# First layer of a two-layer graph transformer: scores by 32-row tiles in four shared PSUM banks, and a new order of the softmax work on VectorE

## The reference

```
q, k, v = x @ wq + bq, x @ wk + bk, x @ wv + bv        # 8 heads of 48
scores  = einsum('bhqd,bhkd->bhqk', q, k) * 48**-0.5 + adj
ctx     = softmax(scores) @ v
x       = rmsnorm(x + ctx @ wo + bo)
x       = rmsnorm(x + silu(x @ w1 + b1) @ w2 + b2)      # 384 -> 1536 -> 384
```

## Time and profile before

| | |
|---|---|
| median of 3 runs | 2001.8 us (2001.61 to 2002.91) |
| profiled execution | 2003.69 us, its span 2001.9 us |
| PE, DVE, ACT, POOL busy | 96%, 67%, 54%, 21% of the span |
| granted TensorE clock, mean | 0.983 |

### The profile page before, as it was taken

The page is one execution under the profiler, slowest core; times in us unless marked ns, Lnnn a source line. Parts: engine busy times, 40 slices in busy tenths (PEclk is TensorE's granted clock), DMA queues, the critical chain, the costliest instruction groups (busy, mean ns, idle before and its releaser), DMA issues.

```text
span 2001.9 us, 50636 instructions
## 1 busy us (share of the span) xinstructions
PE 1928.2 (96%) x18496; PEld 1879.4 (94%) x18496; DVE 1339.1 (67%) x2590; ACT 1088.6 (54%) x2326; POOL 413.6 (21%) x555
## 2 busy tenths in 40 slices
PE   6599999999999999999999999999799999999997
PEld 5589999999999999999999999998799999999997
DVE  6547667766667666676676766764566766666765
ACT  4346555565555655556555565544355555555555
POOL 3011212212112121121211312122122221222222
PEclk9699999999999999999999999999899999999999
DMA  7424444443444444434444344344222222222222
GB/s 191 138 79 119 114 120 121 109 121 111 115 126 108 118 115 112 129 107 119 115 108 133 105 121 115 105 121 111 75 76 87 86 80 71 85 84 87 87 79 65
DMA packets 268645, 213.54 MB, mean 107 GB/s; under 512 B 142784, under 2 KB 251072, under 8 KB 268608
## 3 DMA queue, kind: packets, MB, share of 16 engines
q1 hardware_dynamic: 268608, 213.05, 38.7%
HBM read 120.34 MB, written 79.69 MB: 100 GB/s over the span
## 4 chain that ended last, share of the span: by engine, by line
PE 92%; DVE 3%; DMA 2%; SPq 1%; ACT 1%; issue 1%; POOL 0%; ACTq 0%; POOLq 0%; DVEq 0%
PE a_bank L405 59%; PE b_bank L1243 15%; PE b_banks L1243 5%; PE a_bank L476 3%; PE b_bank L1310 2%; PE a_bank L461 2%; PE b_banks L1297 2%; PE b_banks L1287 2%; PE b_bank L1320 1%; SPq L247 1%; DMA a_hid_stage<-in_L_gnn_w 1%; DMA a_work<-x_turned 1%; DMA x_turned<-a_work 0%; DVE xt_lo L792 0%; DVE a_work L875 0%
## 5 line engine op out<-in xcount | busy, mean ns | idle before, releaser
L405 PE MATMUL a_bank<-a_x1t_hi,a_w_hi 128*128 128x256 f32 x1152 | 329.5, 286 | 9.8 <-DVE a_x1t_lo L807 8.3
L405 PE MATMUL a_bank<-a_x1t_lo,a_w_hi 128*128 128x256 f32 x1152 | 326.2, 283 | 0.0
L405 PE MATMUL a_bank<-a_x1t_hi,a_w_lo 128*128 128x256 f32 x1152 | 326.1, 283 | 0.0
L657 ACT ACTIVATE a_work<-a_bank,a_b 128x256 f32<-128x256 f32 x384 | 159.8, 467 | 240.2 <-PE a_bank L405 239.9
L822 DVE TENSOR_TENSOR a_hid_lo<-a_work,a_hid_hi 128x512 fp32r<-128x512 f32 x192 | 130.8, 694 | 195.3 <-ACT a_hid_hi L662 195.3
L405 PE MATMUL a_bank<-a_w_hi,a_hid_hi 128*128 128x384 f32 x768 | 258.3, 336 | 0.0
L405 PE MATMUL a_bank<-a_w_hi,a_hid_lo 128*128 128x384 f32 x768 | 258.2, 336 | 0.0
L405 PE MATMUL a_bank<-a_w_lo,a_hid_hi 128*128 128x384 f32 x768 | 258.1, 336 | 0.0
L405 PEld LDWEIGHTS a_bank<-a_x1t_hi,a_w_hi 128*128 128x128 f32 x1152 | 219.7, 191 | 18.7 <-issue 9.9
L405 PEld LDWEIGHTS a_bank<-a_x1t_lo,a_w_hi 128*128 128x128 f32 x1152 | 222.5, 193 | 0.0
L405 PEld LDWEIGHTS a_bank<-a_x1t_hi,a_w_lo 128*128 128x128 f32 x1152 | 219.3, 190 | 0.0
(11 more groups left out here) (160 smaller groups left out, 5591.4 us busy)
## 6 DMA issues: line engine op xcount, KB each, us to landing
a_work<-in_x SPq DMA_DIRECT2D x64, 384.0 KB, 3.2
p_turned<-a_work SPq DMA_DIRECT2D x256, 64.0 KB, 1.8
a_work<-p_turned SPq DMA_DIRECT2D x32, 512.0 KB, 3.2
xt_raw<-in_xT SPq DMA_DIRECT2D x32, 384.0 KB, 4.0
ctx_turned<-a_work SPq DMA_DIRECT2D x256, 48.0 KB, 1.7
a_work<-ctx_turned SPq DMA_DIRECT2D x32, 384.0 KB, 3.1
x_turned<-a_work SPq DMA_DIRECT2D x256, 48.0 KB, 1.7
a_work<-x_turned SPq DMA_DIRECT2D x32, 384.0 KB, 3.8
```

The source lines that it names most:

```text
L405: r = pe.matmul(out, lhs[a], rhs[b], start=first and n == 0, stop=last and n == 2)
L657: r = act.activation(silu[:, p % 2, s * GROUP:(s + 1) * GROUP], A[p % 3][:, s * GROUP:(s + 1) * GROUP], ACT.Silu, bias=b1[:, m:m + 1])
```

## The change

PE multiplies the scores in tiles of 32 rows by 64 columns: a head's 48 features are 32 rows of one matmul and 16 rows of another, and the columns of wq and wk are put in that order when they are split at the start. There are 48 matmuls a group in place of 12, each over 32 rows. The four row tiles write to four PSUM banks; these four are shared with the values, the output projection and the sums of `ffn2`. k is kept in four copies in place of ten (DVE writes three, ACT one), and the scale is folded into q.

One semaphore now tells that the scores of both tiles are ready. `soften` is cut in two: `add_adj` (both tiles, which frees the banks) and `shift` (maximum and subtraction). The order on DVE is `take_ctx`, `add_adj` of both tiles, `shift` of tile 0, `turn_ctx`, `shift` of tile 1. At the start the biases go through DRAM so that they stand by row, and the load of wv is issued behind them.

```diff
-        bank = [ctx.enter_context(nc.psum_tensor(f"a_bank{i}", [P, 512], F32)) for i in range(8)]
-        A, B, ACC = bank[0:3], bank[3:6], bank[6:8]
-        V_BANK, PV_BANK, S_BANK, OUT_BANK = (B[0], B[1]), (B[2], B[0]), (B[1], B[2]), (B[0], B[1])
+        A = [ctx.enter_context(nc.psum_tensor(f"a_bank{i}", [P, 512], F32)) for i in range(3)]
+        PV_BANK = (ctx.enter_context(nc.psum_tensor("a_bank3", [P, 512], F32)), A[2])
+        s_banks = ctx.enter_context(nc.psum_tensor("a_banks", [P, ROWS, 512], F32))
+        V_BANK = OUT_BANK = (s_banks[:, 0, :], s_banks[:, 1, :])
+        ACC = (s_banks[:, 2, :], s_banks[:, 3, :])
...
+            load_piece(sp, pieces[0], w_loaded[0], by_block=False)
+            for name in ("bq", "bk"):
+                sp.dma_start(scratch[name].rearrange("(k p) -> p k", p=P), w[name],
+                             allow_slow_non_contiguous=True).then_inc(bias_placed, 16)
...
+            sp.wait_ge(bias_placed, 32)
...
+                for m, part in enumerate((pairs[:, 0:WHOLE], pairs[:, DH0:DH0 + WHOLE], each[:, WHOLE:DH0])):
+                    sp.dma_start(dst[:, m:m + 1], part).then_inc(early_loaded, 16)
             load_piece(sp, pieces[WV], w_loaded[WV], by_block=False)
...
-            def scores(g, t, back):
...
-                for k in range(KT):
-                    b0, b1_, h = SPAN0[k]
-                    for s in range(2):
-                        n = TILES * t + s
-                        r = pe.matmul(S_BANK[t][64 * s:64 * s + 64, h * NODES:(h + b1_ - b0) * NODES],
-                                      q[:, k, n * NODES:(n + 1) * NODES],
-                                      k_blocks[:, n, b0:b1_, :].rearrange("p b n -> p (b n)"),
-                                      start=k == 0, stop=k == KT - 1, skip_group_check=True)
+            def scores(g):
...
+                for t in range(TILES):
+                    for m in (2, 0, 1):
+                        for i in range(ROWS):
+                            row = slice(WHOLE * i, WHOLE * i + WHOLE)
+                            for s in range(2):
+                                nodes = slice((TILES * t + s) * NODES, (TILES * t + s + 1) * NODES)
+                                at, n = (P * t, 2) if m == 2 else (P * t + NODES * m, 1)
+                                r = pe.matmul(s_banks[64 * s:64 * s + 64, i, at:at + n * NODES].rearrange("p (e n) -> p e n", e=n),
+                                              q[row, m, nodes], k_t[row, m:m + n, nodes],
+                                              start=m == 2, stop=m < 2, skip_group_check=True)
                 r.then_inc(s_mm, 1)
...
                 if back:
                     for t in range(TILES):
                         take_ctx(b, t)
+                if new:
+                    for t in range(TILES):
+                        add_adj(g, t)
+                    shift(g, 0)
+                if back:
                     for t in range(TILES):
                         turn_ctx(b, t)
                 if new:
-                    for t in range(TILES):
-                        soften(g, t)
+                    shift(g, 1)
```

More of the change, by code:

```diff
@@ L77, in layer0 @@
     S = H0 * NODES
+    ROWS, WHOLE, PART = 4, 32, DH0 - 32
     with ExitStack() as ctx:
@@ L417, in qk @@
                         pe.wait_ge(*((k_done, g) if u == 0 else (q_done, 2 * (g - 1) + u)))
+                        if u == 2:
+                            wait(pe, ctx_done, TILES * (g - 1))
                     else:
@@ L448, in pv @@
                 pe.wait_ge(v_kept, TILES * g + t + 1)
[L449 to L456, removed]
+                if t == 1:
+                    pe.wait_ge(*((q_done, 2 * (g + 2)) if new else (silu_done, FP * (g - 1))))
                 for h in range(H0 // 2):
@@ L495, in attn_out, with ffn1 @@
                 r.then_inc(o_mm, 1)
-            def ffn1(f, p, new):
+            def ffn1(f, p, new, back):
                 if p == 0:
@@ L506, in ffn1 @@
                 else:
-                    pe.wait_ge(silu_done, FP * f + p - 2)
+                    wait(pe, silu_done, FP * f + p - 2)
+                if p == 2 and back:
+                    pe.wait_ge(ctx_done, TILES * (f + 2))
                 for s in range(2):
@@ L535, in step @@
                 if new:
-                    for t in range(TILES):
-                        scores(g, t, back)
+                    scores(g)
                 ahead = nxt and isinstance(g, int) and g < 3
@@ L544, in step @@
                     for p in range(3):
-                        ffn1(f, p, new)
-                    ffn2(f, 0)
-                    ffn1(f, 3, new)
+                        ffn1(f, p, new, back)
+                    ffn2(f, 0, new)
+                    ffn1(f, 3, new, back)
                     ffn2(f, 1)
@@ L552, in step @@
                 if ffn:
-                    ffn1(f, 4, new)
+                    ffn1(f, 4, new, back)
                     ffn2(f, 2)
-                    ffn1(f, 5, new)
+                    ffn1(f, 5, new, back)
                     for p in range(3, FP):
@@ L579, in high @@
                 act.wait_ge(loaded, count)
-                act.activation(halves(piece, 0), stage(piece), ACT.Copy).then_inc(done, 1)
+                if piece[1] is w["wq"] or piece[1] is w["wk"]:
+                    for m in range(KT):
+                        r = act.activation(by_head(halves(piece, 0), m, False), by_head(stage(piece), m, True), ACT.Copy)
+                    r.then_inc(done, 1)
+                else:
+                    act.activation(halves(piece, 0), stage(piece), ACT.Copy).then_inc(done, 1)
             def w1_high(i):
```

125 lines of the change are left out of this document (69 added, 56 removed).

## The result

The changed kernel takes 2033.0 us (median of 4 runs, 2031.59 to 2034.53) where the kernel before takes 2002.35 (median of 4 runs): ratio 1.0151, 95% interval 1.0137 to 1.0165. The profiled execution has a span of 2029.8 us, 27.9 more than before.

What follows compares the result with a forecast made beforehand. PE was taken to bound the kernel: +12.6 us in the loop, -6.5 in the first steps and +1.3 at the start sum to +7.4 us, 2009.2 us from a median of 2001.8; 8 in 10 range 1982 to 2024.

Steps and rivals of the forecast that it cites:

- the start: Before the first steps: wv, issued behind the biases' round trip through DRAM, comes later; +1.3 us (0 to +3).
- the 27 steps: Steps 4 to 30 of the loop: each longer by 0.45 us because the context comes late, +12.2 us.
- step 31: Last of the steps with all parts: longer by 0.45 us, like the others in the loop.
- the first steps: Steps 1 to 3: scores no longer wait for the context, returning 2.5, 3 and 1 us; -6.5 us (-8 to -4).
- The way of the context: DVE's turns, SP's stores and load up to `attn_out`: turns wait behind a subtraction held by POOL; `attn_out` +0.45 us.
- Two of its signs: Expected in the changed profile: first subtraction 1.3 us long, and PE idle some 1.3 us at `attn_out`'s first matmul.
- The scores: PE's score matmuls in a loop step: 1.36 us instead of 2.26, saving PE 0.90 us (0.57 to 0.99).
- The sign for steps 1 and 2: Expected in the changed profile: in steps 1 and 2 PE starts right after `xt_lo`.
- A full step: A step of the loop: from 41.83 to 42.28 us, +0.45, PE's gain eaten by a wait at `attn_out`.
- The range: Whole kernel: 8 in 10 within 1982 to 2024 us, leaving out the ends of the main case.
- the forecast's own case: Loop: context late, subtraction held by POOL, +0.15 to +1.15 us a step; 1999 to 2025 us, 66%.

Runs made afterwards that it cites:

- e8_pool_behind: Changed kernel with POOL's last pair of additions of a step waiting until both subtractions are done; 2023.7 us, ratio 1.0099.
- e9_no_round_trip: Changed kernel without the biases' way through DRAM, bq and bk loaded as they lie (biases in wrong rows); 2027.3 us, ratio 1.0126.
- e1_pad: Changed kernel with 64 unused bytes a partition ahead of the work tensors, restoring their old addresses; 2031.9 us, ratio 1.0140.
- e10_order_only: Kernel before with only the new order on DVE, scores and k as before; 2023.2 us, ratio 1.0100.
- e3_turn_first: Changed kernel with the turns of the context put back ahead of the two additions on DVE; 1998.2 us, ratio 0.9970.
- e7_best: Changed kernel with turns ahead of the additions, 64 bytes of padding and all early loads ahead of the biases' wait; 1988.7 us, ratio 0.9926.
- e4_stores_behind: Changed kernel with the two bias stores moved behind the loads of wk and wq in SP's queue; 2034.4 us, ratio 1.0158.
- e5_wv_ahead: Changed kernel with the load of wv issued ahead of the wait for the biases; 2033.2 us, ratio 1.0150.
- e11_best2: Changed kernel with turns first, 64 bytes of padding, and biases loaded to SBUF, stored from there, loaded by row ahead of wo and w1; 1979.7 us, ratio 0.9886.

## Why the prediction was wrong

The span missed the forecast by 20.5 us (27.9 less 7.4): the start has 8.4 of them, the 27 steps 8.2, step 31 3.0, the rest 0.8 and the first steps 0.1.

**The way of the context** was right. In us after `pv`: the end of the first subtraction 6.22 forecast (606.42 - 600.20) and 6.2 measured; the load's issue 11.7 and 11.71; `attn_out` 16.82 and 16.86; the mechanism, held by POOL, is shown by e8_pool_behind. Two of its signs came out smaller. The subtraction arrived 0.24 us later than forecast (5.19 after `pv`, not 4.95) and so took 1.02 us instead of 1.3, with the same end, which POOL sets. PE waited 0.93 us in step 14 instead of 1.3, since it asked later: it had gained 0.78, not 0.90, and `ffn1` and `ffn2` ahead of the wait ran slower.

The scores took 1.39 us where 1.36 was forecast, 14.5 ns an instruction of the trace. By the 60 cycles of the Trainium skill (TensorEngine Tiling (Array Packing), Performance Considerations) for each of 96 instructions they would have taken an estimated 2.4 us, which the trace contradicts. But the page speaks of matmuls, and there are 48: counted so, the estimate is 1.2 us, and the trace does not contradict it. So the rule did not speak against the gain as the prediction says.

**The first steps** came to -6.4 for -6.5 by luck, since errors in the parts cancelled: step 1 gave back 3.65 us and step 2 3.46 (2.5 and 3 forecast, 3.2 each called the most), while step 3, where 1 was to come back, took 0.69 longer. The sign for steps 1 and 2 was right: PE starts right after `xt_lo`. In step 3 the wait only moved: PE waits 2.91 us for the low half of x1 ahead of `ffn1`, where before the scores waited 2.65 us for `take_ctx`.

**The start** is the term that failed most: "I count +1.3 us (0 to +3)". It measured +9.7, and e9_no_round_trip gives 9.5 of it to the biases' way. The price of the round trip was taken from the eight large stores of x1, some 5 us until the load's issue; with two stores of 384 single words 10.56 passed from the issue of the second to the next issue behind the wait (2.48 to 13.04). And the prediction looked at SP's queue alone, where the stores stand ahead of wv only in waiting: they also stand ahead of two pieces of wk, which landed after 10.69 us. The Trainium skill (DMA: Bandwidth & Descriptors, Rules for kernel authors) says that a strided last dimension becomes one descriptor for each element; the 10.56 us agree that such a store is slow, and the change had two.

**A full step** was 0.74 us longer (mean of steps 5 to 30) instead of 0.45, in three terms that the runs tell apart: the later `attn_out` 0.47 (0.40 forecast); PE's restart after the wait 0.11 (25.51 us from `attn_out` to `pv` in e1_pad and e10_order_only against 25.41; 0.05 forecast); and 0.16 for the slower matmuls at other addresses (0.20 without a wait, e3_turn_first against e7_best). The prediction has the last at nothing: "Behind `attn_out` PE has its work ready as before". Times 27 it is 4.2 us. The 0.05 came from a wrong reading: the 0.39 us in the earlier trace rows are a first matmul of `ffn1` with 256 columns, which follows the scores without a wait.

**Step 31** had the same mechanism with a worse size: a context later by 1.6 us, 1.1 of them in the landing of the stores, and 1.7 us of matmuls at the lower clock, which a wait in the loop (at most 1.5 us) never caused in this execution. In e4_stores_behind, e5_wv_ahead and e8_pool_behind the wait of this step was 1.6 to 1.7 us and the clock stayed at 1.00. Where the last 0.8 us lie is not known.

**The range** has a sum that is wrong. The bounds given for the forecast's own case, 28 x 1.15 - 4 + 3, make +31 us and so 2033, where the prediction says 2025. That this is the measured time is chance: the start lies far outside its bound of +3, and a step well inside its +1.15.

## What to carry to other kernels

When a step of work is moved ahead of the first link of a chain through DRAM, compare the chain's slack with the whole of the delay, the wait included: here some 2.1 us of slack (the prediction's sum) met 2.4 of delay, and a gain of 0.78 us on the bounding engine became a wait on it. Moving the turns back gave 35 us. A tiny DMA of single words is dear twice, by its own 10 us and by what stands behind it in its queue; take its price from a transfer of the same form, not from one on the same route. After any change of an allocation, compare the distance of equal matmuls in a stretch without waits.

## What the runs showed of the hardware

The time of a matmul depends on where tensors lie in SBUF: the same 84 matmuls took 12.57 or 12.71 us when the work tensors moved by 64 bytes, and whole kernels 1979.7 or 1993.9 us when the padding was 64 or 96 bytes. It is not alignment to 64 bytes: a move by 64 keeps it and changes the time, and 96 bytes put the work tensors at a multiple of 64 and are the slower. It is not the address alone either, since at the same addresses two parts of `ffn1` took 117.7 ns a matmul in the kernel before and 113.3 in e11_best2. Stores of 384 words of 4 bytes took 8.6 to 10 us, from SBUF and from DRAM, where a 48 KB store of the context lands in 1.7 us (page of the changed kernel). A subtraction on DVE with two inputs in SBUF took 0.69 us alone and 1.02 beside POOL's addition.
